# Routed mixture on Trainium2: chunks of two and six sequences instead of four and four, small work moved from GpSimd to VectorE, addresses read earlier

## The reference

```
def _L1_ffn_ref(x, w_gate, w1, w3, w2):
    E, H, TOP_K = (8, 256, 2)
    xt = x.reshape(-1, embed_dim)
    logits = xt @ w_gate
    top_logits, sel = jax.lax.top_k(logits, TOP_K)
    probs = jax.nn.softmax(top_logits, axis=-1)
    h = silu(einsum('td,edh->eth', xt, w1)) * einsum('td,edh->eth', xt, w3)
    y = einsum('eth,ehd->etd', h, w2)
    out = sum over the two chosen experts of their y * prob
...
x = x + _L1_attn_b_ref(_layernorm(x), ...)
x = x + _L1_ffn_ref(_layernorm(x), ...)
```

## Time and profile before

| | us |
|---|---|
| median of three runs | 2675.16 |
| lowest, highest | 2672.88, 2677.55 |
| the profiled execution's own time | 2669.71 |
| its span, first to last instruction | 2667.5 |
| mean granted TensorE clock | 0.894 of full speed |

### The profile page before, as it was taken

How to read it: one execution, slowest core, us unless ns; L and a number is a source line. 1 busy time by engine, 2 the same in 40 slices (tenths; PEclk the granted TensorE clock), 3 DMA queues, 4 the chain that set the end, 5 groups by cost and what they waited for, 6 DMA issues and landing times. The chain is left out here.

```text
span 2667.5 us, 40619 instructions
## 1 busy us (share of the span) xinstructions
PE 2200.5 (82%) x11840; PEld 1315.8 (49%) x11840; DVE 1647.1 (62%) x4376; ACT 1278.4 (48%) x2252; POOL 1448.1 (54%) x1499
## 2 busy tenths in 40 slices
PE   4577997998779889989999945776999999954766
PEld 3345564666656556644444433544444444433544
DVE  6865775776667657756666633435787787733424
ACT  4642454332435433336666523432677677642433
POOL 5923654443256533446666655744676666535743
PEclk8687898998979999989999957887999999966888
DMA  1001111222011122210000032232000000021224
GB/s 49 0 3 29 37 37 50 83 86 82 1 41 37 25 90 96 88 62 1 1 1 1 1 89 62 59 92 79 0 1 1 1 0 1 1 77 51 67 69 133
DMA packets 106948, 112.44 MB, mean 42 GB/s; under 512 B 21816, under 2 KB 86200, under 8 KB 106488
## 3 DMA queue, kind: packets, MB, share of 16 engines
q1 hardware_dynamic: 97656, 91.08, 11.6%
q0 software_dynamic: 9088, 18.89, 2.2%
HBM read 71.91 MB, written 25.29 MB: 36 GB/s over the span
## 5 line engine op out<-in xcount | busy, mean ns | idle before, releaser
L2330 DVE TENSOR_REDUCE l_diffneg_max<-psum 128x1 fp32r<-128x512 f32 x512 | 335.5, 685 | 92.7 <-PE psum L2068 86.6
L2245 ACT ACTIVATE l_diffweights<-psum 128x1024 f32<-128x1024 f32 x256 | 262.0, 1026 | 128.9 <-PE psum L2097 127.9
L2068 PE MATMUL psum<-l_diffkz,l_diffQ 128*128 128x512 f32 (+1 forms) x512 | 235.2, 478 | 3.2 <-DVE l_diffneg_max L2330 2.1
L5034 POOL DMA_INDIRECT results<-l_moe1y,l_moe1xt x156 | 151.8, 973 | 149.1 <-DVE l_moe1y L4944 129.6
L2869 ACT ACTIVATE l_lightswapped<-psum 32x512 f32<-32x512 f32 x304 | 179.0, 589 | 101.1 <-DVE l_lightturned L2961 97.7
L1595 DVE TENSOR_REDUCE l_attn0neg_max<-psum 128x1 fp32r<-128x512 f32 x256 | 167.2, 683 | 54.0 <-PE psum L1329 51.3
L4710 PE MATMUL psum<-l_moe1w,l_moe1zt 128*128 x312 | 186.2, 681 | 9.1 <-ACT l_moe1zt L4790 6.3
L1501 ACT ACTIVATE l_attn0weights<-psum 128x1024 f32<-128x1024 f32 x128 | 130.2, 1023 | 120.7 <-PE psum L1351 120.6
L174 POOL TENSOR_TENSOR settled<-powers 128x1 f32<-128x1 f32 x113 | 27.5, 244 | 294.1 <-DVE l_alibimv L701 69.6
L1722 POOL TENSOR_TENSOR l_attn0half_sums<-l_attn0weights 128x2048 f32<-128x2048 f32 x30 | 137.1, 4571 | 89.6 <-ACT l_attn0weights L1501 89.6
L4294 ACT ACTIVATE l_moe0s<-psum 128x512 f32<-128x512 f32 x144 | 85.8, 596 | 198.4 <-PE psum L854 173.9
(11 more groups left out here) (606 smaller groups left out, 6109.8 us busy)
## 6 DMA issues: line engine op xcount, KB each, us to landing
l_moe0bcs<-gate_rows SPq DMA_DIRECT2D x64, 512.0 KB, 4.4
l_moe1xt<-sorted SPq DMA_DIRECT2D x156, 66.0 KB, 1.8
l_attn0Q<-l_attn0q_hi SPq DMA_DIRECT2D x128, 64.0 KB
l_moe1yb<-results SPq DMA_DIRECT2D x32, 256.0 KB, 3.3
l_moe1w<-in_moe_w SPq DMA_DIRECT2D x6, 1024.0 KB, 8.3
l_attn0Q<-l_attn0q_lo SPq DMA_DIRECT2D x64, 64.0 KB
l_moe0w_raw<-in_moe_w SPq DMA_DIRECT2D x20, 128.0 KB, 4.7
results<-l_moe1y,l_moe1xt POOLq DMA_INDIRECT x156, 2.2
```

What stands on the lines that cost most here:

```text
L2068: nc.tensor.matmul(ps[:, bank, :], Q[rows, n % 4, st * P:(st + 1) * P], kz[rows, n % 4, hh, :], start=True, stop=True).then_inc(pe_max.sem ...
L2245: nc.scalar.activation(weights[:, tt, 2 * pair:2 * pair + 2, :], ps[:, S[m % 2]:S[m % 2] + 2, :], ACT.Exp, scale=SCALE).then_inc(act_exp.s ...
L2330: nc.vector.tensor_reduce(neg_max[:, n % 2, st, row:row + 1], ps[:, bank_of(("max", n, b)), :], AXX, ALU.max, negate=True).then_inc(vec_ma ...
L5034: p.indirect_dma_start(core.dram["results"], bass.IndirectOffsetOnAxis(ap=xt[:, n % SLOTS, R.DEST:R.DEST + 1].bitcast(U32), axis=0), y[:, ...
```

## The change

It does five things. (1) Chunks of two and six sequences, with 23 and 55 tiles. (2) Sequences begin six steps apart instead of eight; steps for which the first chunk has no turns left (25 to 43) run after its turns, alone. (3) GpSimd keeps only the power of the scale; variance plus epsilon and the shift are made on VectorE, the shift of a layer's first sequence with no power; the destinations of all sequences are made once at the layer's start by one iota and copied into the rows by VectorE among the weights. (4) The address of tile i+1 is read behind the up product of tile i. (5) The turns of a chunk are one fewer, with nothing in the one left out but empty steps.

```diff
-    SEQS = 4
-    CHUNKS = NSEQ // SEQS
-    TILES = SEQS * NQ * 2 + 7
-    REGION = SEQS * NQ + 1
+    SEQS = (2, 6)
+    CHUNKS = len(SEQS)
+    FIRST = [0, *accumulate(SEQS)][:CHUNKS]
+    TILES = [seqs * NQ * 2 + 7 for seqs in SEQS]
+    FIRST_TILE = [0, *accumulate(TILES)][:CHUNKS]
+    MOST = max(TILES)
+    REGION = max(SEQS) * NQ + 1
...
-    APART, SPAN = 8, 10
+    APART, SPAN = 6, 10
...
-        PREPARE = APART * (R.SEQS - 1) + SPAN + 4
-        TURNS = range(R.TILES + 3)
+        prepare_steps = lambda c: range(APART * (R.SEQS[c] - 1) + SPAN + 4)
+        turns = lambda c: range(R.TILES[c] + 2)
+        spare_turns = lambda c: [k for k in prepare_steps(c + 1) if k not in turns(c)] if c + 1 < R.CHUNKS else []
...
@@ tensor
-            for k in range(PREPARE):
+            for k in prepare_steps(0):
                 prepare(0, k)
...
+                expert_of = lambda i: t.value_load(table[0:1, c, W_AT + i:W_AT + i + 1], min_val=0, max_val=7 * R.COLS)
                 wait(t, vec_table, c, "pads")
-                at_w = {}
+                at_w = {0: expert_of(0)}
                 tile_turned(n0)
                 tile_turned(n0 + 1)
-                for i in TURNS:
-                    if i < R.TILES:
-                        at_w[i] = t.value_load(table[0:1, c, W_AT + i:W_AT + i + 1], min_val=0, max_val=7 * R.COLS)
+                for i in turns(c):
+                    if i < R.TILES[c]:
                         up(n0 + i, at_w[i])
-                    if 0 <= i - 2 < R.TILES:
+                    if i + 1 < R.TILES[c]:
+                        at_w[i + 1] = expert_of(i + 1)
+                    if 0 <= i - 2 < R.TILES[c]:
                         down(n0 + i - 2, at_w.pop(i - 2))
...
+                for k in spare_turns(c):
+                    prepare(c + 1, k)
@@ scalar
-                wait(a, pool_scale, j, "shift")
+                wait(a, vec_shift, j, "shift")
@@ vector
-                wait(d, pool_scale, j - 2, "shift")
+                wait(d, vec_shift, j - 2, "shift")
...
+                wait(d, vec_stats, j, "mean", NQ - 1)
+                settle(core, d)
+                wait(d, pool_scale, j - 2, "scale")
+                inc(v.tensor_scalar(var[:, j % 2, :], mv[:, j % 2, :, 1], LN_EPS, None, ALU.add), "var")
+
+            def shifted(j):
+                vec_shift.start()
+                if j:
+                    wait(d, pool_scale, j, "scale")
+                wait(d, act_z, j - 2, "again")
+                v.scalar_tensor_tensor(shift[:, j % 2, :], moments(j)[:, :, 0], -1.0, scale_of(j)[:, :], ALU.mult, ALU.mult
+                                       ).then_inc(vec_shift.sem, vec_shift.step("shift"))
...
+                inc(v.tensor_copy(rows[:, j % 2, :, :, R.DEST].bitcast(U32), dest[:, :, j, :]), "to")
...
+                if due(c, k, 1) is not None:
+                    shifted(due(c, k, 1))
@@ gpsimd
+            nc.gpsimd.iota(dest[:, :, :, :].rearrange("p k j q -> p (k j q)"), [[P, 2 * NSEQ * NQ]], 0, 1).then_inc(counted, 1)
...
             def token_scale(j):
                 pool_scale.start()
-                if j:
-                    wait(p, vec_stats, j, "mean", NQ - 1)
-                wait(p, act_z, j - 1, "again")
-                settle(core, p)
-                inc(nc.gpsimd.tensor_scalar(minus[:, :], moments(j)[:, :, 0], -1.0, None, ALU.mult), "minus_mean")
-                inc(nc.gpsimd.tensor_scalar(var[:, :], moments(j)[:, :, 1], LN_EPS, None, ALU.add), "var")
-                wait_for("var")
-                inc(nc.gpsimd.tensor_tensor(scale[:, :], var[:, :], core.half, ALU.pow), "scale")
-                wait_for("scale")
-                inc(nc.gpsimd.tensor_tensor(shift[:, :], minus[:, :], scale[:, :], ALU.mult), "shift")
-
-            def destinations(j):
-                pool_dest.start()
-                if j >= 2:
-                    rows_sorted(p, j - 2)
-                for k in range(2):
-                    nc.gpsimd.iota(rows[:, j % 2, k, :, R.DEST].bitcast(I32), [[P, NQ]], k * NSEQ * T + j * T, 1
-                                   ).then_inc(pool_dest.sem, pool_dest.step("to", k))
+                wait(p, vec_stats, j, "var")
+                wait(p, vec_shift, j - 2, "shift")
+                wait(p, act_z, j - 2, "again")
+                nc.gpsimd.tensor_tensor(scale[:, j % 2, :], var[:, j % 2, :], core.half, ALU.pow
+                                        ).then_inc(pool_scale.sem, pool_scale.step("scale"))
```

More of the change, by code:

```diff
@@ L13 @@
 from contextlib import ExitStack
+from itertools import accumulate
 import math
@@ L4530, in routed_block @@
     SLOTS, YS = 10, 4
-    APART, SPAN = 8, 10
+    ROW_AT, W_AT, PAD_AT = 0, 64, 128
+    APART, SPAN = 6, 10
     COMBINE, BETWEEN = 16, 4
-    N = R.CHUNKS * R.TILES
-    chunk_of = lambda j: j // R.SEQS
-    last_of = lambda c: (c + 1) * R.SEQS - 1
+    chunk_of = lambda j: max(c for c in range(R.CHUNKS) if R.FIRST[c] <= j)
+    last_of = lambda c: R.FIRST[c] + R.SEQS[c] - 1
     with ExitStack() as ctx:
@@ L4572, in routed_block @@
         opening = core.opening
-        for of in (vec_stats, pe_tr, act_hi, vec_lo):
+        for of in (vec_stats, pool_scale, pe_tr, act_hi, vec_lo):
             of.skip_first()
@@ L4636, in all_results @@
             def all_results(c):
-                for n in range((c + 1) * R.TILES - YS, (c + 1) * R.TILES):
+                for n in range(R.FIRST_TILE[c] + R.TILES[c] - YS, R.FIRST_TILE[c] + R.TILES[c]):
                     result_out(sp, n)
@@ L4808, in prepare @@
                     head_hi(due(c, k, 4))
-            for k in range(PREPARE):
+            for k in prepare_steps(0):
                 prepare(0, k)
             for c in range(R.CHUNKS):
-                n0 = c * R.TILES
+                n0 = R.FIRST_TILE[c]
                 tile_turned(n0)
                 tile_turned(n0 + 1)
-                for i in TURNS:
-                    if i < R.TILES:
+                for i in turns(c):
+                    if i < R.TILES[c]:
                         silu(n0 + i)
-                    if i + 2 < R.TILES:
+                    if i + 2 < R.TILES[c]:
@@ L4837, in _ @@
-            v.tensor_copy(base[:, :], small[:, 40:48]).then_inc(fixed, 1)
+            v.tensor_copy(tix[:, :], small[:, 0:R.MOST]).then_inc(fixed, 1)
+            v.tensor_copy(base[:, :], small[:, 64:72]).then_inc(fixed, 1)
             v.memset(one8[:, :], 1.0).then_inc(fixed, 1)
             v.memset(spare[:, :, 0:R.DEST], 0.0).then_inc(fixed, 1)
-            v.tensor_copy(spare[:, :, R.DEST].bitcast(U32), small[:, 48:48 + 8 + R.SPARES]).then_inc(fixed, 1)
+            v.tensor_copy(spare[:, :, R.DEST].bitcast(U32), small[:, 72:72 + 8 + R.SPARES]).then_inc(fixed, 1)
@@ L5037, in prepare @@
             def prepare(c, k):
-                if due(c, k, 1) is not None:
+                if due(c, k, 1):
                     token_scale(due(c, k, 1))
-                    destinations(due(c, k, 1))
                 if due(c, k, 7) is not None:
```

114 lines of the change are left out of this document (58 added, 56 removed).

## The result

The changed kernel takes 2662.19 us (median of 20 runs, 2651.71 to 2673.51); the kernel before took 2673.60 us beside it (20 runs, 2666.49 to 2692.22). The ratio is 0.9949, 95% interval 0.9934 to 0.9965: 13.6 us faster (9.4 to 17.6); the two medians alone are 11.4 apart.

A forecast was written before the change was run, and what follows sets the result against it. GpSimd was taken to bound the routed layers' first chunk, TensorE the second. A to D summed to -4.8 us (eighth layer) and -1.5 (tenth), together -6.3: median 2668.9, stated as 2669; range 2648 to 2691, own range 2660 to 2678.

The forecast's parts named there:

- A: First preparation of each routed layer, two sequences instead of four: first table sooner, -35 us per layer.
- B: From the first chunk's first y to the second chunk's first y: +6.1 us (eighth layer) and +8.0 (tenth).
- C: Second chunk, 55 tiles instead of 39, turns of 1.68 us through the early read: +19.1 and +19.7 us.
- D: Tail of each routed layer, six sequences' sums instead of four after the last result: +5.0 and +5.8 us.
- y1: The y of tile 1, first in a layer's first chunk: forecast about 46 us after the layer's start.
- E: End of a sequence's last sort on GpSimd; ScalarE's wait then holds GpSimd's next result until 7.1 us later.
- bare steps: Preparation steps with no turns beside them: forecast 12.9 us each instead of 15.8.
- Small work: Three operations per sequence moved to VectorE, 0.2 us each: hidden by GpSimd in the dense stretch, 10 us without cover.
- Rival 1: First chunk: ScalarE's wait for the sorts costs nothing; -18 us, 2651; chance 22%.
- Rival 2: Second chunk: the turn stays at 1.87 us, the read now delaying the down product; +20 us, 2689; chance 18%.
- Rival 3: Preparation does not overlap as worked out, spare steps take 15.8 us: +19 at most, 2679; 15% shared with Rival 4.
- Rival 4: The split only moves the wait: first table 35 us sooner, all given back; near the forecast; 15% shared with Rival 3.

The follow-up runs named there:

- Experiment 2: The changed kernel with only the early address read undone; 2693.80 us, ratio 1.0052.
- experiment 4: The changed kernel with chunks of four and four sequences, eight steps apart; 2665.98 us, ratio 0.9955.
- experiment 8: The kernel of experiment 4 with the shift issued behind the placing on VectorE instead of ahead of it; 2650.83 us, ratio 0.9889.
- experiment 6: The changed kernel with three buffers of sorted rows and row addresses instead of two; 2643.79 us, ratio 0.9845.
- experiment 1: The kernel before with only the early read: tile i+1's address read behind the up product of tile i; 2654.07 us, ratio 0.9924.
- experiment 9: The kernel of experiment 6 with six buffers for the sums and the stores of x behind all reads; 2636.13 us, ratio 0.9846.

## Why the prediction was right, and where its sizes were off

**The sum.** Predicted -6.3 us, measured by stages -15.8, by the runs -13.6 (9.4 to 17.6). The time lay in the forecast's own range of 2660 to 2678. By terms, both layers together: A -71.6 (predicted -70), B +9.5 (+14.1), C +34.8 (+38.8), D +11.5 (+10.8). The differences are -1.6, -4.6, -4.0 and +0.7, together -9.5: two terms of the sum mis-sized, B and C, each within its bounds over the two layers; no step of the mechanism fell. But the error of the sum is larger than the change of 6.3 that it forecast. That B and C both erred to the slow side kept the sign; this much of the hit was luck.

**A, right.** The first table comes 24.8 / 24.4 us behind the start (24.4 predicted), y1 45.9 / 44.8 (46). From the table to y1 are 21.2 / 20.4 us, not the unchanged 21.9; what is known of it stands under B.

**B, the mechanism right, the size 4.6 us too large.** Against y1 the sorts of the three sequences that end in the turns end at 40.1, 63.7 and 86.4 us in the eighth layer (predicted 39.9, 64.5, 87.9). The wait appears where it was put, but one period costs 23.6 and the next 22.7 instead of 24.7. From E to GpSimd's next result are 6.8 us instead of 7.1, and from there to the next E 16.9 instead of 17.6: scale and second-power follow each other in 2.04 us, for which 2.4 were taken. The bare steps are 13.2 us on average, not 12.9. The last sequence is placed at y1 + 113.0 (113.7), its table is there at 117.0 (117.3), and from there to the first y are 20.1 us, not 21.5. That last 1.4 was carried over from before without asking what the edit does to it: the table to the first y also holds reads of addresses, which no longer stand ahead of every up product. Experiment 2, with the read put back, has 20.7 / 20.9 us there, and 21.9 / 21.0 from the first table to y1. So the read accounts for 0.6 to 0.8 us at each of the four places; the other 0.6 to 0.8 of B's 1.4 stay open.

**C, the mechanism right, the size 4.0 us too large.** The turn is 1.66 us in the eighth layer, between the bound of 1.64 and the 1.68 taken, and 1.63 in the tenth, just under the bound. The guess kept part of the 0.10 us by which an up product that had stood idle is longer (1.12 in the earlier trace rows, 1.02 now); it goes with the idling entirely. In the eighth layer a turn is 0.03 us longer than in the tenth; in its second chunk the next layer is prepared too, which is argued as the cause and not shown. The prediction's doubt, that the read would now delay the down product, is settled by the timeline: down starts 0.86 us behind up in the turns shown, with a read of 0.30 to 0.36 us in front of it, as it did before (2578.38 to 2579.24).

The Trainium skill, page "DMA: Bandwidth & Descriptors", section "Latency and other measured facts", would have the read at 600 ns at least. Here the measurement decides: the 156 reads from the table have a median of 0.30 us. What experiment 2 loses by the read, 26.9 us over 156 up products, is 0.17 us each, and 0.22 us a turn in the second chunks.

**D, right:** 4.9 and 6.5 (predicted 5.0 and 5.8).

**Small work: whether "about nothing" holds in this kernel is not shown,** as no run has six steps apart without it. At eight steps apart it costs 5.4 us (experiment 4), through a wait at the head of VectorE's step; experiment 8 shows that wait. At six apart the shift and the placing fall into different steps, 1 and 9 behind the start against a distance of six, so that the wait with the placing behind it, at least, cannot arise. The prediction counted three operations of 0.2 us and did not ask what stands behind them in the list, though the change adds a wait there.

**Rival 1 (ScalarE's wait costs nothing, 2651)** fell: the wait costs 21.6 us (experiment 6). Its price in the prediction, 18, was for the periods, which give 13.6, and left out the bare steps, which give 6.1. A kernel without the wait is experiment 6, ratio 0.9845, or 2634 us against the 2675.16 from which the rival's 2651 was worked out. **Rival 2 (the turn stays at 1.87, 2689)** fell as a forecast, but experiment 2 is its number: ratio 1.0052, again 2689 against 2675.16. **Rival 3** fell by A and by bare steps of 13 us. **Rival 4, that the split itself only moves the wait, is what the runs show:** by the layers 5.2 us slower at six apart, 14.6 at eight, 2.8 at six with three buffers. The prediction's sum contained this without saying it: by its own bounds the read was worth 20 us, so that the change without it stood at +14. Measured, it stands at +11.1 by the layers. The gain was forecast with the right sign, but described as a balance of large terms, when it was one edit's.

**Left open.** Why TensorE's clock is granted differently in the ninth layer from profile to profile; why the eighth layer begins up to 9 us apart (1542.25 in experiment 1's profile, 1550.81 after); what limits the reads in the tail of experiment 9.

## What to carry to other kernels

Price a register read by what stands behind it in the queue, not by its own 0.3 us: placed ahead of the matmul that needs it, it cost 0.2 us in every turn of the second chunk, and it went away by being issued one turn earlier. When a change bundles edits, write a sum for each alone: here two edits gave 18.7 and 7.7 us by the layers, two others gave back 10.6, and the bundle hid it. Compare stages of the layers that were edited: an untouched layer alone varied by 16 us between profiles, more than the whole change. And before sequences are moved closer together, ask which buffer they will wait for: one more buffer of rows was worth 21.6 us. The best split found, three and five, at 56 us below the kernel before, was tried only with it.
